# Cosformer attention as causal products of two heads on 64-row tiles, cross attention 1 on the context in SBUF, and two changes of order in a twelve-layer decoder on one Trainium2 core

## The reference

```python
# layer 0 (L0_attn): causal softmax attention, 16 heads of 8, rotary positions
scores = jnp.where(causal, jnp.einsum('bhqd,bhkd->bhqk', q, k) * scale, -jnp.inf)
out = jnp.einsum('bhqk,bhkd->bhqd', softmax(scores), v)
# layer 3 (L1_attn): cosformer, 16 heads of 64, D_MODEL 128, a scan over time
Qp, Kp = relu(x @ Wq + bq), relu(x @ Wk + bk); V = x @ Wv + bv
angles = math.pi / (2.0 * Tlen) * jnp.arange(Tlen)
Qc, Qs, Kc, Ks = Qp * cos(angles), Qp * sin(angles), Kp * cos(angles), Kp * sin(angles)
def step(carry, inp):
    S_cos = S_cos + kc[..., :, None] * v[..., None, :]      # and S_sin with ks_
    z_cos = z_cos + kc                                      # and z_sin with ks_
    num = einsum('bhi,bhij->bhj', qc, S_cos) + einsum('bhi,bhij->bhj', qs, S_sin)
    den = jnp.maximum(jnp.sum(qc * z_cos + qs * z_sin, axis=-1), 1e-06)
    return ..., num / den
return out @ Wo + bo
# layer 4 (L1_xattn): one head of 128, no mask, no output weight
query = hidden_states @ Wq; key, value = jnp.split(decoder_hidden_states @ Wkv, 2, axis=-1)
w = jax.nn.softmax(jnp.einsum('bqd,bkd->bqk', query, key) / sqrt(d), axis=-1)
return jnp.einsum('bqk,bkd->bqd', w, value)
# layer 7 (L2_xattn): 16 heads of 8, sigmoid in place of softmax
scores = jax.nn.sigmoid(jnp.einsum('blhd,bshd->bhls', q, k))
o = jnp.einsum('bhls,bshd->blhd', scores, v)
```

## Time and profile before

| what | value |
|---|---|
| median of 3 runs | 6629.19 us (6628.73 to 6637.26) |
| profiled execution | 6633.89 us, of which span 6632.2 us |
| mean granted PE clock | 0.913 of 2.4 GHz |
| PE busy | 5589.4 us (84%) |
| DVE busy | 3190.2 us (48%) |
| ACT busy | 3158.4 us (48%) |
| POOL busy | 1927.5 us (29%) |

### The profile page before, as it was taken

One profiled execution on the slowest core, in us unless ns is written; L12 is line 12 of the kernel. 1 busy time (PEld: TensorE's weight loads), 2 busy tenths in 40 slices (PEclk: granted clock), 3 DMA queues, 4 the chain that ended last, 5 costly groups with the idle time before them and its releaser, 6 DMA issues. The chain is left out here.

```text
span 6632.2 us, 72209 instructions
## 1 busy us (share of the span) xinstructions
PE 5589.4 (84%) x28734; PEld 1898.4 (29%) x28749; DVE 3190.2 (48%) x4058; ACT 3158.4 (48%) x3282; POOL 1927.5 (29%) x928
## 2 busy tenths in 40 slices
PE   6759998999999999889869559999885388888879
PEld 2213333333333333246624221111242011111123
DVE  6575455555545552124363340000136889998713
ACT  3214444444444445422202239999412067777752
POOL 1007787878778789700000000000000000000000
PEclk7759999999999999999989779999698589999979
DMA  1000000000000000000021030000012100000001
GB/s 39 13 0 1 1 1 1 1 1 1 1 1 1 1 1 1 18 13 7 16 88 36 18 105 17 9 17 2 10 35 92 37 7 12 10 10 10 2 18 32
DMA packets 90077, 113.73 MB, mean 17 GB/s; under 512 B 22782, under 2 KB 66152, under 8 KB 88140
## 3 DMA queue, kind: packets, MB, share of 16 engines
q1 hardware_dynamic: 89740, 109.10, 5.2%
HBM read 73.77 MB, written 35.30 MB: 16 GB/s over the span
## 5 line engine op out<-in xcount | busy, mean ns | idle before, releaser
L2827 DVE TENSOR_REDUCE red<-ps 128x2 f32<-128x1024 f32 (+1 forms) x832 | 976.9, 1182 | 967.6 <-PE ps L2645 965.5
L2764 ACT ACTIVATE Pr<-ps,key_bias 128x1024 f32<-128x1024 f32 x816 | 897.5, 1114 | 1114.1 <-PE ps L2660 1113.6
L2884 POOL TENSOR_TENSOR Ps<-Ps,Pr 128x1024 f32<-128x1024 f32 x400 | 944.2, 2361 | 321.0 <-ACT Pr L2764 321.0
L3320 DVE TENSOR_REDUCE red<-ps 128x2 f32<-128x1024 f32 (+2 forms) x1102 | 961.5, 926 | 81.0 <-PE ps L3235 67.7
L2893 POOL TENSOR_TENSOR Ps<-Ps,Pr 128x1024 f32<-128x1024 f32 x400 | 948.2, 2371 | 32.7 <-ACT Pr L2764 32.7
L492 POOL MEMSET sel<- 16x2048 f32 (+1 forms) x2 | 2.7, 1368 | 3244.2 <-POOLq L89 3244.2
L3298 ACT ACTIVATE Pr<-ps 128x1024 f32<-128x1024 f32 x816 | 786.3, 1021 | 228.2 <-PE ps L3245 227.4
L2658 PE MATMUL ps<-Q,Kr 64*128 64x512 f32 x3264 | 852.8, 601 | 0.0
L2677 PE MATMUL ps<-Pr,Vc 128*64 128x512 f32 x3264 | 789.8, 605 | 0.0
L3421 ACT ACTIVATE Pr<-ps 128x1536 f32<-128x1536 f32 x544 | 732.7, 1495 | 3.9 <-PE ps L3387 3.5
L3235 PE MATMUL ps<-Kp,Q 52*128 52x512 bf16 (+1 forms) x1664 | 450.3, 410 | 225.1 <-DVE red L3320 149.0
(11 more groups left out here) (567 smaller groups left out, 5626.9 us busy)
## 6 DMA issues: line engine op xcount, KB each, us to landing
L_dram_K<-parts SPq DMA_DIRECT2D x26, 384.0 KB, 2.7
Kp<-L_dram_K SPq DMA_DIRECT2D x16, 624.0 KB
L_dram_K<-parts SPq DMA_DIRECT2D x26, 256.0 KB, 2.3
Kp<-L_dram_K SPq DMA_DIRECT2D x16, 416.0 KB
w<-L_ffn_experts_w_dram SPq DMA_DIRECT2D x24, 256.0 KB, 3.0
L_dram_V<-Vt SPq DMA_DIRECT2D x13, 258.0 KB, 3.1
Vc<-L_dram_V SPq DMA_DIRECT2D x13, 258.0 KB, 2.6
ctx<-ctx_dram SPq DMA_DIRECT2D x13, 256.0 KB, 5.8
```

What stands on the lines that cost most here:

```text
L2764: nc.scalar.activation(Pr[:, t % 4, half].rearrange("p a n -> p (a n)"), ps[:, 2 * half:2 * half + 2, :].rearrange("p a n -> p (a n)"), AC ...
L2827: nc.vector.tensor_reduce(red[:, g % 2, q, :], ps[:, maxima_bank(g, q):maxima_bank(g, q) + 2, 0:ctx.keys_in(g % C)], AX, ALU.max).then_inc ...
L2884: nc.gpsimd.tensor_tensor(into, into, src, ALU.add).then_inc(*summed0.up())
L3320: nc.vector.tensor_reduce(red_flat[:, g % 2, first:first + n], ps[:, b:b + n, 0:ctx.keys_in(g % C)], AX, ALU.max).then_inc(*reduced.up())
```

## The change

1. **Layer 3** is rewritten. `cosformer` now works on eight pairs of heads. The relu of queries and keys is kept without the cos and sin parts; scores of the two heads are products over 64 rows each, on rows 0 to 63 and 64 to 127, into two banks; DVE multiplies both by `table`, which holds cos of the difference of the positions and zeros above the diagonal. Values are the weights (128 keys x 64) and scores the moving data, on columns 0 to 63 and 64 to 127 of bank 6 + c, so outputs stand by feature and need no transposes. POOL adds the scores of a pair over key tiles; PE sums them over keys (`add_up`), DVE inverts, PE spreads them (`spread_out`), DVE scales, PE applies the output weight (`output`), all in banks 4 and 5, while the next pair runs. All weights are loaded whole at the start.
2. **Layer 4** is rewritten. `cross_1` folds Wk into the query (`wkT`), so the context in SBUF is the key, and nothing goes through DRAM. Two query halves of 512 run over pairs of key tiles; the maxima of half 1 are taken during half 0. POOL adds up the exponentials.
3. **Layer 0**: the plan puts two score units of a key tile behind each other, with the maxima ahead of both.
4. **Layer 7**: units are four and three banks in turn, over banks 0 to 6; the output gathers in bank 7 for every pair; `Pr` has 21 slots.
5. The context is also kept where layer 4 runs, which changes nothing with all layers on.

`output_projection`, `causal_products`, `rotated`, `Cross`, `mask_rows`, `keys_and_values`, `queries`, `cross_heads`, `bring_together` and `cross_layer` are gone.

```diff
@@ cosformer @@
+    P, d, PER = 8, 64, 12
+    cs = k.load(stack, table_in, "cs", io["cosformer_table"])
+    wq, wk, wv = (k.load(stack, arrived, n, io["L1_attn_" + n]) for n in ("Wq", "Wk", "Wv"))
+    bv = k.load(stack, arrived, "bv", io["L1_attn_bv_row"].to_broadcast([128, P * 128]), [128, P * 128])
+    units = [(0, kt) for kt in range(4)] + [(1, kt) for kt in range(8)]
...
+        for half, sl in enumerate(HALVES):
+            nc.tensor.wait_ge(*made.at(2))
+            nc.tensor.matmul(ps[:, 6 + half, :], lhsT=one_row[:], rhs=cs[:, sl], start=True, stop=True).then_inc(*table_mm.up())
...
+    constants()
+    normed = layer_norm(k, X, h, tmp)
...
+        def queries(p):
+            take(4, q_set.at(p + 1))
...
+        def scores(n):
+            p, c, kt, q, width = unit(n)
+            b = 2 * (n % 2)
...
+            take(b, weighted.at(n + 1))
+            for a in range(2):
+                mm = nc.tensor.matmul(ps[:, b + a, 0:width], lhsT=K[head(a), p % 2, kt * 128:(kt + 1) * 128], rhs=Q[head(a), p % 2, q:q + width], start=True, stop=True)
+            mm.then_inc(*scored.up())
...
+            nc.tensor.wait_ge(*weighted.at(n + 1))
...
+            for a in range(2):
+                at = p * 128 + 64 * a
+                mm = nc.tensor.matmul(ps[head(a), 6 + c, q - HALF * c:HALF], lhsT=V[:, kt, at:at + 64], rhs=Pr[:, n % 6, a, 0:width], start=False, stop=True, skip_group_check=True)
+            mm.then_inc(*weighed.up())
...
+        for n in range(N):
+            p, u = n // PER, n % PER
+            scores(n)
+            if p + 1 < P and u == 0:
+                queries(p + 1)
+            if p + 1 < P and u == 2:
+                keys(p + 1)
+            if p == 0 and u in (4, 6, 8, 10):
+                values(4 + (u - 4) // 2, 4)
+            if p and u == 4:
+                add_up(p - 1)
+            if p and u == 9:
+                spread_out(p - 1)
+            if p and u == 11:
+                output(p - 1)
+            if n >= 2:
+                products(n - 2)
...
+        for n in range(N):                                   # dve
+            p, c, kt, q, width = unit(n)
+            u, b, x0 = n % PER, 2 * (n % 2), q - 128 * kt
+            nc.vector.wait_ge(*scored.at(n + 1))
+            if n >= 6:
+                nc.vector.wait_ge(*weighed.at(n - 5))
+                nc.vector.wait_ge(*summed.at(n - 5))
+            nc.vector.tensor_tensor(Pr[:, n % 6, :, 0:width], ps[:, b:b + 2, 0:width], table[:, x0:x0 + width].unsqueeze(1).to_broadcast([128, 2, width]), ALU.mult).then_inc(*weighted.up())
...
+            if p and u == 4:
+                bound(p - 1)
+            if p and 5 <= u < 9:
+                invert(p - 1, u - 5)
+            if p and u == 10:
+                scale(p - 1)
+            if p >= 2 and u == 0:
+                add_output(p - 2)
@@ causal_attention @@
-        for x, u in enumerate(s_of[b]):
-            if x < n - 3:
-                plan += [("maxima", m) for m in ms[len(ms) * x // (n - 3):len(ms) * (x + 1) // (n - 3)]]
-            if x == n - 2 and b < 7:
+        for x in range(0, n, 2):
+            if x < n - 2:
+                plan += [("maxima", m) for m in ms[len(ms) * x // (n - 2):len(ms) * (x + 2) // (n - 2)]]
+            elif b < 7:
                 plan.append(("turn", b + 1))
-            plan.append(("scores", u))
+            plan += [("scores", s_of[b][x]), ("scores", s_of[b][x + 1])]
@@ cross_1 @@
+        def scores(n):
+            half, u = n // U, n % U
+            take(2 * (n % 2), exp_done.at(n + 1))
+            for x, kt in enumerate(tiles[u]):
+                r = rows_of(kt)
+                nc.tensor.matmul(ps[0:r, 2 * (n % 2) + x, :], lhsT=ctx.t[:, kt * 128:kt * 128 + r], rhs=Q[:, HALVES[half]], start=True, stop=False)
...
+                mm = nc.tensor.matmul(ps[0:r, 2 * (n % 2) + x, :], lhsT=ones[:, 0:r], rhs=Qa[:, half, :], start=False, stop=True)
...
+        for m in range(M):
+            maxima(m)
+            for f in range(len(groups) * m // M, len(groups) * (m + 1) // M):
+                values(f)
...
+        for n in range(2 * U):
+            half, u = n // U, n % U
+            if n == 0:
+                rows(0)
+            scores(n)
+            if half == 0:
+                for m in range(M + M * u // (U - 3), M + min(M, M * (u + 1) // (U - 3))):
+                    maxima(m)
+                if u == U - 2:
+                    rows(1)
+            if n:
+                products(n - 1)
+            if half == 1 and u == 0:
+                sums(0, False)
+                sums(0, True)
+        sums(1, False)
+        sums(1, True)
+        products(2 * U - 1)
@@ small_sigmoid @@
-    U = -(-4 * T // 3)
+    first = lambda u: 7 * (u // 2) + 4 * (u % 2)
+    unit_of = lambda i: 2 * (i // 7) + (i % 7 >= 4)
+    U = unit_of(4 * T - 1) + 1
...
-                if p >= 2:
-                    nc.tensor.wait_ge(*out_copied.at(p - 1))
-                nc.tensor.matmul(ps[:, 6 + p % 2, :], lhsT=zero_row[:, 0:128], rhs=zero_row[:], start=True, stop=True, skip_group_check=True)
+                if p:
+                    nc.tensor.wait_ge(*out_copied.at(p))
+                nc.tensor.matmul(ps[:, 7, :], lhsT=zero_row[:, 0:128], rhs=zero_row[:], start=True, stop=True, skip_group_check=True)
```

More of the change, by code:

```diff
@@ L663, in ffn_experts @@
     experts_dve()
[L666 to L706, removed]
 def values_by_token(k, h, w, heads, dv, V, after):
@@ L917, in cosformer @@
-    h, tmp = k.tile(stack, "h", [D, S]), k.tile(stack, "tmp", [D, S])
-    V = k.tile(stack, "V", [128, TOK_TILES, H, d + 1])
-    O = k.tile(stack, "O", [128, TOK_TILES, H * d])
-    nc.gpsimd.memset(V[:, :, :, d:d + 1], 1.0).then_inc(*ones_set.up())
-    normed = layer_norm(k, X, h, tmp)
-    values = values_by_token(k, h, wv, H, d, V, [arrived.all(), normed[0], normed[1]])
-    def row_pe():
-        for c in range(2):
-            nc.tensor.matmul(ps[:, c, :], lhsT=k.consts.ones[0:1, :], rhs=bv[0:1, c * HALF:(c + 1) * HALF], start=True, stop=True).then_inc(*row_mm.up())
@@ new lines, in cosformer, with unit, constants @@
+    zero_row = k.tile(stack, "zero_row", [1, HALF], BF16)
+    head = lambda a: slice(64 * a, 64 * a + 64)
+    units = [(0, kt) for kt in range(4)] + [(1, kt) for kt in range(8)]
+    N = P * PER
+    def unit(n):
+        c, kt = units[n % PER]
+        q = max(HALF * c, 128 * kt)
+        return n // PER, c, kt, q, HALF * (c + 1) - q
+    def constants():
+        p = nc.gpsimd
+        p.memset(one_row[:], 0.0)
+        p.memset(spread[:], 0.0)
+        p.memset(ones[:], 1.0)
+        p.memset(zero_row[:], 0.0).then_inc(*made.up())
+        p.wait_ge(*made.at(1))
+        for c in range(2):
+            for a in range(2):
+                at = 32 * (2 * c + a)
+                p.memset(spread[at:at + 1, c, head(a)], 1.0)
+        p.wait_ge(*table_in.dmas(1))
+        for row in (0, 64):
+            copied = p.tensor_copy(one_row[row:row + 1, :], cs[row:row + 1, 0:128])
+        copied.then_inc(*made.up())
+        for half, sl in enumerate(HALVES):
+            nc.tensor.wait_ge(*made.at(2))
+            nc.tensor.matmul(ps[:, 6 + half, :], lhsT=one_row[:], rhs=cs[:, sl], start=True, stop=True).then_inc(*table_mm.up())
+        nc.scalar.wait_ge(*table_mm.at(2))
+        nc.scalar.copy(table[:], ps[:, 6:8, :].rearrange("p a n -> p (a n)")).then_inc(*table_scaled.up())
+        p.wait_ge(*table_scaled.at(1))
+        p.affine_select(out=table[:, 0:128], in_=table[:, 0:128], compare_op=ALU.is_ge, fill=0.0, base=0, pattern=[[1, 128]], channel_multiplier=-1).then_inc(*table_set.up())
@@ L948, in retention @@
+    pe()
+    act()
+    pool()
+    dve()
+    k.barrier(table_in, arrived)
 def retention(k, io, X, stack):
@@ L1494, in pe @@
                 scores(n, u % 3)
-                while 2 * done + 1 <= n - 2:
+                while n % 2 == 1 and 2 * done + 1 <= n - 2:
                     products(done)
@@ L3406, in pe @@
             scores(u)
-            while done < T and (4 * done + 3) // 3 <= u - 2:
+            while done < T and unit_of(4 * done + 3) <= u - 2:
                 products(done)
```

1157 lines of the change are left out of this document (348 added, 809 removed).

## The result

The changed kernel takes 6390.7 us (median of 4 runs, 6383.97 to 6406.36), the one before 6629.9 us in its 4 runs; the ratio is 0.964 with a 95% interval of 0.9621 to 0.9659. That is 239 us less where 260 were forecast, and 6390.7 lies in the range of 6320 to 6415. The profiled execution took 6391.8 us with a span of 6390.0.

A forecast was written before the change was run, and what follows sets the result against it. PE was taken to bound layer 3 and layer 4's main run, ACT layer 7, nothing layer 0. Layers 3, 4, 7 and 0 sum as -121 - 129 - 5 - 5 = -260, giving 6370 us, range 6320 to 6415.

The forecast's parts named there:

- The switch of tiling: Layer 3, PE changing between score and product rows: 0.25 us per unit, bounds nothing and 0.35; 3.0 us per pair.
- The wait at the queries: Layer 3, pairs 2 to 6: PE stands 2.5 to 2.8 us until DVE has added an earlier output to X.
- the first pair: Layer 3, pair 0: eight value products and no sums, 30.2 us.
- The start: Layer 3, before the pairs: cs copies and spreading, queries and keys, eight value products, low clock at first; 33 us.
- Layer 4: Making of keys, half of the maxima's own time and the DRAM way at the end go: 275 us, -129.
- Layer 7: Sigmoid loop: 467 activations for 544, saving 0.066 us fixed part each; -5 us, range -6 to +2.
- Layer 0: Score rows in twos may let two halves of the array work together; -5 us, range -20 to +10.
- Cheap tiles: Layer 3 rival: tiling switches lie under the next row's fill, waits hidden; -46 us, about 6323; chance 0.12.
- The scratch chain: Layer 3 rival: banks 4 and 5 wait at each handover, pairs of 35 us; +28, 6398 us; chance 0.20.
- The port: Layer 3 rival: DVE multiplications wait for POOL additions, pairs of 36 or 37 us; +54, 6424 us; chance 0.04.
- The clock as the sign-changing case: Layers 3 and 4 rival: new loops granted 1.2 GHz, 452 us more, 6821; slower below 0.64; chance 0.02.

The follow-up runs named there:

- the twos: Changed kernel with layer 3 running two score rows, then two product rows, spread and output behind the products: 6371.5 us, ratio 0.9603.

## Why the prediction was right, and where it was off

Place and sign of every term were right, and the time lay in the range, in its upper part. Part of that nearness is luck: layers 0 and 7 gave 9 us more than forecast for reasons that the forecast did not have, and hid as much of what was missing in layers 3 and 4. By size the terms went as follows.

**The switch of tiling** (the change between score rows and product rows) was the term of layer 3 that was mis-sized. The forecast took 0.25 us per unit and kept 0.35 as its bound; measured is 2.07 - 1.72 = 0.35. The row of layer 9 had it right, and I leaned on layer 1, where a bf16 product in the score row's tiling hides how long the way back takes. 12 x 0.10 is 1.2 us a pair and shows nearly alone in pair 1, which does not wait at the queries: 30.08 against 29.0. Eight pairs make 9.6 us.

**The wait at the queries** was right: five pairs, released by DVE's addition, 2.45 us against 2.5 to 2.8, and 0.42 and 0.58 for spread and output against 0.5 and 0.7. What the forecast left out is **what a wait does to the clock**. It treated the granted clock as one rival for the layer, with a chance of 0.02, and not as part of a wait's price. In each of five pairs the queries behind the wait took 3.51 in place of 1.98 us, 7.7 us in all, and the last spread and output 3.75 and 3.64 in place of 1.96, 3.5 us. The rows were there to be read: layer 3's first products stood behind 9.07 us of waiting, and the start was even costed at a low clock, but nothing of it was applied further in.

The three, 9.6 + 7.7 + 3.5 = 20.8, are nearly all of the 22 us; the rest lies in the first pair (32.85 against 30.2, of which 1.2 are the switch). The start, 33.5, was forecast at 33.

**Layer 4** came to 280.7 us against 275: the maxima of half 1 were costed by PE's time alone, with DVE's reductions called hidden. On average they are, but two in a row share one pair of banks, and that cost some 7 us. **Layer 7** got 8 us, not 5: the fixed part was near (3.9 against 5), the late starts weren't in the sum. **Layer 0** was inside its range of -20 to +10, but for another reason than the term's: it was built on the overlap of two units, and at like clock the two orders took nearly the same time.

**The rivals.** Cheap tiles: refuted, by 0.35 and by the gain of the twos. The scratch chain would have made pairs of 35 with waits at keys, spread and output; pairs were 34.1, near it, but for other reasons: keys never waited, and spread and output together 1.0 us. Anyone who had looked at the pair's length alone would have taken this rival for confirmed. The port: refuted. DVE's multiplications ran at their usual length beside POOL's additions:

```profile
L948 DVE TENSOR_TENSOR Pr<-ps,table 128x1024 f32<-128x1024 f32 x48 | 57.9, 1206 | 45.1 <-PE ps L796 45.1
```

There are 48 of them at 1206 ns, with POOL busy for 136.2 us of the layer on 80 additions. Half of the 48 had a POOL addition beside them for all or most of their time and took 1.16 to 1.23 us, the other half had none and took 1.22 to 1.23. The Trainium skill (SBUF - State Buffer, Who interferes with whom) says that a VectorE instruction with at most one input in SBUF does not contend with GpSimd, outside of certain fast modes. The trace agrees with that. The clock as the sign-changing case did not come: 0.93 over layer 3 and 0.97 over layer 4, far above 0.64.

## What to carry to other kernels

Price a wait of TensorE with what it does to the clock: at the queries a wait of 2.45 us cost 4.0, one of 1.81 only itself, and the cure was to change the place of one addition on another engine. The length alone is no rule, since in layer 0 a wait of 2.46 us cost no clock; look at the granted clock behind each. Where rows of one tiling alternate with rows of another, put two of a kind behind each other; with the waits that went along it took 2.7 us of 30 from a pair here. And compare layers, not totals, when part of a kernel runs at a clock that changes from execution to execution.

## What the runs showed that was not expected

Behind ten products of one row, 2.2 us with PE busy throughout, the clock was at 0.50; four passes over all 128 rows in the same wait kept it at full speed. Work of no use, put into a wait, made layer 3 shorter by 7.0 us in one case and by 3.4 in the other.

The price of changing the tiling stands in two places. In the changed kernel's records the last pass of a row is followed by the first of another tiling after 0.53 us (0.43 where the tiling stays). The second pass behind a change starts 0.53 after the first in a score row and 0.48 in a product row (again 0.43 where the tiling stays). The Trainium skill says that a change of mode drains TensorE (TensorEngine Tiling (Array Packing), Key Properties), without a price. Here it is 0.15 to 0.20 us, 0.18 on average.
